# Moving key norms and norm ends from VectorE to ScalarE and GpSimd, and dealing decoding anew, in a two-layer decoder kernel

## What is computed

```python
# blocks 1 and 2: linear attention, then a selective scan gated by x
x = _layernorm(x + _L0_attn_ref(x, ...), axis=-1)
x = _layernorm(x + _L0_xattn_ref(ctx_1024, x, ...), axis=-1)   # y * silu(x)
# block 5: cross attention, 16 heads of 128
q = rmsnorm((hidden_states @ Wq).reshape(B, Sq, H, D), gq)
k = rmsnorm((encoder_hidden_states @ Wk).reshape(B, Skv, H, D), gk)
v = (encoder_hidden_states @ Wv).reshape(B, Skv, H, D)
attn = jax.nn.softmax(jnp.einsum('bqhd,bkhd->bhqk', q, k) * scale, axis=-1)
out = jnp.einsum('bhqk,bkhd->bqhd', attn, v).reshape(B, Sq, H * D) @ Wo
# block 6: feed forward whose weights are lut[idx], lut of 16 values
```

## Time and profile before

| | us |
|---|---|
| median of 3 runs | 2836.32 |
| the runs | 2829.55, 2836.32, 2836.57 |
| the profiled execution | 2836.43 |
| its span, first to last instruction | 2834.7 |
| PE busy | 2579.2 (91%) |
| DVE busy | 2044.9 (72%) |
| ACT busy | 1207.1 (43%) |
| POOL busy | 705.2 (25%) |

### The profile page before, as it was taken

The page is one execution under the profiler, slowest core; times in us unless marked ns, Lnnn a source line. Parts: engine busy times, 40 slices in busy tenths (PEclk is TensorE's granted clock), DMA queues, the critical chain, the costliest instruction groups (busy, mean ns, idle before and its releaser), DMA issues. The chain is left out here.

```text
span 2834.7 us, 29502 instructions
## 1 busy us (share of the span) xinstructions
PE 2579.2 (91%) x9938; PEld 1707.4 (60%) x9938; DVE 2044.9 (72%) x3585; ACT 1207.1 (43%) x2171; POOL 705.2 (25%) x617
## 2 busy tenths in 40 slices
PE   6998898989789789789899999999999997999997
PEld 2343433434367555566667776777777774588886
DVE  3879999899975377687868897889878895231332
ACT  3453544634433221356554555465645564021111
POOL 1445445456401156211111220111111110000000
PEclk8989999999989899899999999999999998999999
DMA  4111211112311202322323223322323215100000
GB/s 147 52 46 61 67 65 61 53 37 74 113 58 40 87 30 75 119 100 102 130 71 114 77 79 108 123 75 86 105 71 120 82 46 172 60 9 22 31 15 15
DMA packets 81568, 212.47 MB, mean 75 GB/s; under 512 B 8966, under 2 KB 17414, under 8 KB 77324
## 3 DMA queue, kind: packets, MB, share of 16 engines
q1 hardware_dynamic: 72108, 178.25, 19.0%
q0 software_dynamic: 5472, 21.01, 1.9%
q10 hardware_dynamic: 3840, 11.34, 1.1%
HBM read 164.11 MB, written 46.47 MB: 74 GB/s over the span
## 5 line engine op out<-in xcount | busy, mean ns | idle before, releaser
L2327 POOL TENSOR_TENSOR h<-du,Bb 128x1024 f32<-128x1024 f32 x128 | 312.7, 2445 | 242.6 <-DVE h L1785 240.5
L1780 DVE TENSOR_TENSOR_SCAN h<-bank,h 128x512 f32<-128x512 f32 x256 | 300.0, 1208 | 39.7 <-ACT bank L1366 32.2
L1366 ACT ACTIVATE bank<-dt,A 128x512 f32<-128x512 f32 x256 | 175.6, 690 | 317.8 <-DVE h L1780 317.1
L1554 ACT ACTIVATE p<-bank,sm,rq 128x512 f32<-128x512 f32 x256 | 199.1, 778 | 223.6 <-DVE sm L2198 223.6
L2401 POOL TENSOR_TENSOR rq<-rq,mhalf 128x4 f32<-128x4 f32 x64 | 79.4, 1241 | 819.1 <-DVE rq L2142 819.1
L694 PE MATMUL bank<-pT,v 128*128 128x512 f32 x512 | 231.2, 594 | 0.8 <-ACT pT L1257 0.8
L279 POOL TENSOR_SCALAR rstd<-mv 128x1 f32<-128x1 f32 x96 | 29.9, 312 | 788.2 <-DVE mv L273 788.2
L908 PE MATMUL bank<-h,ident 128*128 128x512 f32 x256 | 148.6, 664 | 53.9 <-DVE h L1785 53.5
L2281 DVE TENSOR_TENSOR h<-bank,sg 128x512 f32<-128x512 f32 (+1 forms) x44 | 30.4, 690 | 228.5 <-PE bank L1205 228.5
L1034 PE MATMUL bank<-x_hi,wxq_s 128*128 128x512 f32 x512 | 169.9, 414 | 23.7 <-DVE wxq_s L2154 22.0
L2194 DVE TENSOR_REDUCE sm<-bank 128x1 f32<-128x512 f32 x256 | 175.0, 684 | 7.6 <-PE bank L1034 7.4
(11 more groups left out here) (248 smaller groups left out, 6081.8 us busy)
## 6 DMA issues: line engine op xcount, KB each, us to landing
wxq_s<-wq_dram SPq DMA_DIRECT2D x48, 512.0 KB, 4.0
Bb<-bc_dram SPq DMA_DIRECT2D x32, 512.0 KB, 3.7
Cb<-bc_dram SPq DMA_DIRECT2D x32, 512.0 KB, 3.7
x_dram<-xo POOLq DMA_DIRECT2D x16, 1024.0 KB, 4.9
xc<-x_dram SPq DMA_DIRECT2D x16, 1024.0 KB, 5.3
woh<-in_Wo SPq DMA_DIRECT2D x64, 256.0 KB, 2.7
wxv_s<-wkv_dram SPq DMA_DIRECT2D x12, 1024.0 KB, 4.9
wxk_s<-wkv_dram SPq DMA_DIRECT2D x12, 1024.0 KB, 8.1
```

Of the source, the lines that this page charges most:

```text
L1366: act.activation(bank[2 + n][:, :], dt[:, c % 2, et, :], ACT.Exp, scale=A[:, et, 2 * w + n:2 * w + n + 1]).then_inc(dA_ready, 1)
L1554: act.activation(p4[:, t, :], bank[4 + t][:, :], ACT.Exp, bias=sm4[:, 4 + t:5 + t], scale=rq[:, hh % 2, 1, t:t + 1], accum_out=sm4[:, 8 + ...
L1780: dve.tensor_tensor_scan(h[:, s, n, :], bank[2 + n][:, :], h[:, s, n, :], 0.0, ALU.mult, ALU.add).then_inc(scanned, 1)
L2327: pool.tensor_tensor(h[:, G % HR, :, :], du[:, et:et + 1, :].to_broadcast([P, 2, S]), Bb[:, w % 2, :, :], ALU.mult).then_inc(dBu_ready, 1)
```

## The change

Three things are changed.

First, `key_norms` leaves DVE. ACT makes the squares with `key_squares`, one activation for each head's 128 columns of a key tile (16 for a group), each with an accumulated sum into `kss`, after all key tiles of the call are brought; a ring of six buffers takes the squares themselves. POOL adds the epsilon ahead of its power.

Second, in the heads of stage 3 the remainders of Wq, Wv and Wk in chunk 0 come ahead of the decoding, and all decoding comes behind `k_rest` and `query_mean`: masks and first pair in hh % 4 = 0; second, third, fourth pair and the next unit's masks in 1; all four pairs of the second unit in 2; none in 3. In PE's output pass `query_squares` moves from head 10 to head 11.

Third, in stage 0 `last` and `last_gated` of the chunks 0 to 2, and `last` of chunk 3, move to ACT as an Identity activation with scale and bias, at other units; POOL makes the bias by one more product (`ln_pool_shift`). The gated norm of the last chunk stays on DVE.

```diff
...
         mv = sb("mv", [P, 2, 2])
-        rstd = sb("rstd", [P, 2, 2])
+        rstd = sb("rstd", [P, 2, 4])
         mhalf = sb("mhalf", [P, 16])
...
         ln_rstd = sem("ln_rstd")
+        ln_shift = sem("ln_shift")
         ln_out = sem("ln_out")
...
+        def ln_pool_shift(pool, T, k, S):
+
+            ln_pool(pool, T, k)
+            pool.wait_ge(ln_rstd, START + T + 1)
+            hold(pool)
+            pool.tensor_scalar(rstd[:, k, 2:3], mv[:, k, 0:1], rstd[:, k, 0:1], -1.0, ALU.mult, ALU.mult).then_inc(ln_shift, 1)
+
+        def ln_last_act(act, S, k, dst):
+
+            act.wait_ge(ln_shift, START + S + 1)
+            act.activation(dst, rsum[:, k, :], ACT.Identity, scale=rstd[:, k, 0:1], bias=rstd[:, k, 2:3]).then_inc(ln_out, 1)
+
         def ln_last(dve, T, k, dst):
...
         pT = s4("pT", [P, NT, S])
-        sm4 = s4("sm4", [P, 16])
+        sm4 = s4("sm4", [P, 16]); kj = s4("kj", [P, 6, XD])
 
...
                             turn_keys(c + 1, 0)
+                        if hh == 11:
                             query_squares(c + 1, 0)
...
                 act.activation(one_e[:, :, :], one_e[:, :, :], ACT.Ln).then_inc(sp_l, 1)
+
+            def last(c, t):
+
+                act.wait_ge(stored, STORED0 + 16 * c)
+                ln_last_act(act, 8 * c + t, t % 2, x1[:, t, :])
+
+            def last_gated(c, t):
+
+                ln_last_act(act, 8 * c + 4 + t, t % 2, xo[:, t, :])
 
...
                         else:
+                            if U == 3 and c:
+                                last_gated(c - 1, 0)
+                                last_gated(c - 1, 1)
+                            if U == 5 and c:
+                                last_gated(c - 1, 2)
+                                last_gated(c - 1, 3)
+                            if U in range(28, 32):
+                                last(c, U - 28)
                             if U == 3:
...
+                        def key_squares(c, g, tiles):
+                            act.wait_ge(k_pow, START + after(c, 16, 4 * g))
+                            for t in tiles:
+                                act.wait_ge(a_done, evicted4(c, "k", g, t))
+                                for n in range(4):
+                                    m = after(c, 4 * 16, 16 * g + 4 * t + n)
+                                    act.wait_ge(k_sum, START + max(0, m - 5))
+                                    act.activation(kj[:, m % 6, :], kt4[:, t, n * XD:(n + 1) * XD], ACT.Square, scale=float(XD) ** -0.5,
+                                                   accum_out=kss[:, t, n:n + 1]).then_inc(k_sum, 1)
+
                         def values(c, g):
...
                             keys(0, 0, range(NT))
+                            key_squares(0, 0, range(NT))
                             values(0, 0)
...
                                 keys(c, hh // 4 + 1, range(NT))
+                                key_squares(c, hh // 4 + 1, range(NT))
                             if hh == 12 and c + 1 < B:
...
                                 round_out(hh)
+                                if 3 <= hh < 7:
+                                    key_squares(c + 1, 0, (hh - 3,))
                                 if hh == 10:
...
-            def last(c, t):
-                dve.wait_ge(stored, STORED0 + 16 * c)
-                ln_last(dve, after(c, 8, t), t % 2, x1[:, t, :])
-
             def gated(c):
...
                         first_gated(c - 1, 1)
-                    if U == 2 and c:
-                        last_gated(c - 1, 0)
-                        last_gated(c - 1, 1)
                     if U == 3 and c:
...
                         first_gated(c - 1, 3)
-                    if U == 4 and c:
-                        last_gated(c - 1, 2)
-                        last_gated(c - 1, 3)
                     if U == 3:
...
                         first(c, U - 26)
-                    if U in range(27, 31):
-                        last(c, U - 27)
             gated(B - 1)
...
-                        def key_norms(c, g, tiles):
-
-                            for t in tiles:
-                                n = 4 * g + t
-                                dve.wait_ge(a_done, evicted4(c, "k", g, t))
-                                dve.wait_ge(k_sum, START + after(c, 16, max(0, n - 1)))
-                                dve.wait_ge(ln_out, START + T0[3] + after(c if g else max(0, c - 1), 4, 0))
-                                dve.tensor_tensor(rsum[:, t % 2, :], kt4[:, t, :], kt4[:, t, :], ALU.mult).then_inc(k_square, 1)
-                                dve.wait_ge(k_square, START + after(c, 16, n + 1))
-                                dve.tensor_reduce(kss[:, t, :], rsum[:, t % 2, :].rearrange("p (n d) -> p n d", d=XD), AX.X, ALU.add)\
-                                    .then_inc(k_sum, 1)
-                                dve.wait_ge(k_sum, START + after(c, 16, n + 1))
-                                dve.tensor_scalar(kss[:, t, :], kss[:, t, :], 1.0 / XD, LN_EPS, ALU.mult, ALU.add).then_inc(k_mean, 1)
-
                         def key_scale(c, g):
...
                             wxq_rest(1)
-                            key_norms(0, 0, range(NT))
                             x3_rest(0, range(KD))
...
                                 q_rest(c, hh + 1)
-                            if hh % 4 == 0:
-                                masks(n)
-                            if hh % 4 == 2 and two:
-                                second_pair(n + 1)
                             if hh + 1 < XH:
...
                                 query_mean(c, hh + 1)
+                            if c == 0 and hh + 2 < XH:
+                                wxq_rest(hh + 2)
+                            if c == 0 and hh % 4 == 0 and hh // 4 + 1 < GROUPS:
+                                wxv_rest(hh // 4 + 1)
+                            if c == 0 and hh % 4 == 1 and hh // 4 + 1 < GROUPS:
+                                wxk_rest(hh // 4 + 1)
                             if hh % 4 == 0:
+                                masks(n)
                                 first_pair(n)
+                            if hh % 4 == 1:
                                 second_pair(n)
-                            if hh % 4 == 1:
                                 third_pair(n)
...
                                 masks(n + 1)
+                            if hh % 4 == 2 and two:
                                 first_pair(n + 1)
-                            if hh % 4 == 2 and two:
+                                second_pair(n + 1)
                                 third_pair(n + 1)
-                            if hh % 4 == 3 and two:
                                 fourth_pair(n + 1)
-                            if c == 0 and hh % 4 == 0 and hh // 4 + 1 < GROUPS:
-                                wxv_rest(hh // 4 + 1)
-                            if c == 0 and hh % 4 == 1 and hh // 4 + 1 < GROUPS:
-                                wxk_rest(hh // 4 + 1)
-                            if c == 0 and hh + 2 < XH:
-                                wxq_rest(hh + 2)
-                            if hh % 4 == 2 and hh // 4 < 3:
-                                key_norms(c, hh // 4 + 1, range(NT))
                             if hh == 12 and c + 1 < B:
...
                                     x3_rest(c + 1, (2, 3))
-                                if 3 <= hh < 7:
-                                    key_norms(c + 1, 0, (hh - 3,))
                                 if hh == 7:
...
                     if U in (29, 30, 31):
-                        ln_pool(pool, after(c, 8, U - 29), (U - 29) % 2)
+                        ln_pool_shift(pool, after(c, 8, U - 29), (U - 29) % 2, 8 * c + U - 29)
                     if U == 0 and c:
-                        ln_pool(pool, after(c - 1, 8, 3), 1)
+                        ln_pool_shift(pool, after(c - 1, 8, 3), 1, 8 * (c - 1) + 3)
                     if U in (4, 6) and c:
-                        ln_pool(pool, after(c - 1, 8, U), 0)
-                        ln_pool(pool, after(c - 1, 8, U + 1), 1)
+                        ln_pool_shift(pool, after(c - 1, 8, U), 0, 8 * (c - 1) + U)
+                        ln_pool_shift(pool, after(c - 1, 8, U + 1), 1, 8 * (c - 1) + U + 1)
                     if U == 8 and c:
...
                         inputs(c + 1, et)
-            for t in range(3, 8):
+            ln_pool_shift(pool, after(B - 1, 8, 3), 1, 8 * (B - 1) + 3)
+            for t in range(4, 8):
                 ln_pool(pool, after(B - 1, 8, t), t % 2)
...
                 for t in range(NT):
+                    pool.wait_ge(k_sum, START + 4 * after(c, 16, 4 * g + t + 1))
+                    hold(pool)
+                    pool.tensor_scalar(kss[:, t, :], kss[:, t, :], LN_EPS, None, ALU.add).then_inc(k_mean, 1)
                     pool.wait_ge(k_mean, START + after(c, 16, 4 * g + t + 1))
```

## The result

| | before | after |
|---|---|---|
| median of 13 runs each, us | 2832.3 | 2843.62 |
| lowest to highest | 2824.17 to 2839.29 | 2828.25 to 2849.98 |
| profiled execution's span | 2834.7 | 2845.1 |

The changed kernel takes 1.0044 of the time of the one before, 95% interval [1.0027, 1.0061]: slower by 0.44%, 11 us. The forecast was 2848.5, in a range of 2822 to 2868.

The account below looks back on a forecast made before the run. In chunks 1 to 3 PE was taken as nearly full, 59.5 of 62.8 us a group. Terms -14.6 + 2.2 - 12 + 19.8 + 17.8 - 1 = +12.2 on 2836.32 gave 2848.5 us, range 2822 to 2868.

Parts of the forecast that it names:

- key path not late: Rival, cross attention: POOL's four powers end before T+8.7, so the detour is gone; -20.6, 2816 us; chance 0.24.
- T+8.7: 8.7 us after head 7's first score (T): previous end of the fourth key_scale product, deciding whether POOL's powers come late.
- the nine groups: Groups with keys in chunks 1 to 3: later transposes and half clock cost 2.2 us each, +19.8 (+5 to +35).
- the first stage: Norm ends moved off DVE there: -14.6 us (-20 to -4).
- 1.8 a tile: POOL's addition plus power per key tile in cross attention: 1.8 us against 1.42, fourth power ending at T+9.45.
- the start of the stage: Cross stage start: 16 squares stand on ACT ahead of values and rounding of x, +2.2 us (0 to +5).
- The rival's reward: Cross attention: DVE, 6.2 us lighter, has q_lo ready when PE asks; 1.5 us a group gained, 13 in the sum.
- Part 2, tails: Last groups of chunks 1 to 3, decoding dealt anew: +7.3 in chunk 3, +5.8, +3.2, clock +1.5; +17.8 (+11 to +24).
- In heads 0 to 11 this fits: Cross attention: decoding behind k_rest fits before PE wants the next weights; heads with values or keys allow 9.6 to 9.9 us.
- Chunk 0: Its heads in cross attention: remainders ahead of decoding remove 22.0 us of PE waits; net -12 us (-20 to -4).
- the pairs' 4.8 a chunk: First stage, gated norm ends off DVE: PE starts keys 3.0 us sooner at upper clock, 4.8 a chunk, -14.4 in all.
- the boundaries: First stage chunk boundaries: one more product in ACT's chain, +1.3 us in the first, -0.25 in two, +0.8 in all.

Follow-up runs that it names:

- part 3 alone: Kernel before with only the first stage's norm ends moved to ACT and POOL; median 2817.9 us, ratio 0.9938 [0.9916, 0.9960].

## Why the prediction was right, and where it was not

**Direction and size** came out (11 us slower against 12), and of the rivals "key path not late" came nearest in its condition (its four powers did end before T+8.7), but not in its time. That the size fits is luck: the nine groups came out 10.9 below their forecast, the first stage gained 8.0 less than its forecast, the last groups cost 3.9 more than theirs, and these and smaller errors cancelled. What was right in the mechanism is the price of the new deal in the last heads.

**Part 1, the step that failed** is the term "1.8 a tile", POOL's pace. I took 1.26 to 1.42 for a power from the earlier trace rows, where four powers stood beside DVE's norms; in this head they took 1.53 once and 1.03 three times, the addition 0.22 rather than 0.33. The fourth power came at T+8.0 instead of T+9.45, below the stated T+8.7, so the +19.8 was not owed. The squares (0.33 forecast, 0.29 measured) and the start of the stage (+2.2) were right. The rival's reward, 13 us, was wrong as well: with powers at T+8.0 DVE's fourth product ends where it did, so nothing is late and nothing is gained.

**Part 2, tails**: +17.8 forecast, +21.7 measured; putting the old deal back there alone gave 22 by timing and 20.7 by the groups, chunk 0 included. The mechanism was the one named. In chunk 3 DVE's way from the end of `q_lo` to the maxima of head 15 grew by 6.4 us (5.4 to 11.8; forecast 5.4 and 1.2, 6.6), and heads 12 and 13 added 0.8 and 1.8. **Heads 0 to 11** is the second step that failed: "In heads 0 to 11 this fits". I compared decoding with PE's room in the head and left out that in heads 3, 7 and 11 four `key_scale` products stand between the maxima and the weights. The 9.9 us of head 2, 6 and 10 leave no room, the maxima come 0.9 late, and PE, which already waited 1.5 there, waits longer and drops to the lower clock. It cost +8.9 in these nine groups. This error hid the first one.

**Chunk 0**: -12 forecast, -11.3 measured, of parts that were not forecast so: -17.5 for the remainders (measured alone), +8.9 for the deal, and -2.6 without a cause shown.

**Part 3**: the pairs' 4.8 a chunk was right (4.9). The step that failed is the boundaries, "+0.8": they cost 5.7. The prediction named the longer chain on ACT but put it at 1.3 once and -0.25 twice; it was 1.9 to 2.0 each time, and ACT's wait for POOL's bias ahead of the fourth norm end (2.55 in chunk 1) was not in the sum. How much of the first stage's -14.6 was wrong stays open: by spans it is -6.6, by timing part 3 alone gives -17.5 (11 to 24) and the gated ends alone 0.70% [0.45, 0.95].

## What to carry to other kernels

Where two engines meet at a point, compute when each arrives, and price what is queued between that engine's inputs and the point: here four products between maxima and weights turned a deal that fits PE's time in the head into a late one. Work taken off an engine that is not last is worth nothing (key norms), however many microseconds it frees, and it costs where the engine that takes it over is last (ungated norm ends, 1.9 at each boundary), while the order of what is left on it was worth 39 us one way and 17 the other. Take the price of an instruction from rows where its neighbours are those that it will have.

## What the runs showed of the hardware

A DVE product of two SBUF operands that meets a POOL product lasts until 1.08 us after POOL's ends, in all 73 that took 1.30 or more in the two kernels; the others take 1.22 to 1.30.

A power of 128x4 on POOL took from 1.03 to 1.53 us in one head: 1.53 beside DVE's predicated copies and first maximum, 1.03 beside its maxima and products. In the kernel before all 56 powers of 1.24 to 1.27 lay beside decoding and all 36 of 1.42 to 1.45 beside the key norms. In the kernel with the key norms alone moved it took 1.32 where it began beside a product of DVE's. What sets this I did not find out.

The same program can pass one place at either clock level. The changed kernel and the one with the norm ends alone have the same first stage; window by window (length, busy PE, PEld, DVE, ACT, POOL, PEclk, DMA share, GB/s), the changed kernel and then the other:

```profile
180.00:190.00 10.00, 10.00 (x13) 3.21 (x12) 4.55 (x4) 3.69 (x6) 3.90 (x2) 0.57 0.00 0
```

```profile
180.00:190.00 10.00, 8.81 (x20) 3.57 (x21) 9.66 (x11) 6.66 (x9) 6.10 (x3) 1.00 0.36 106
```

At 0.57 chunk 0 of that stage took 184.6 us, at 1.00 176.9. From 169 to 190 us the granted clock was 0.59 in the changed kernel and in the one before, and 1.00 in the one with the norm ends alone; in the 6 us ahead of it PE had been busy 5.67 in all three. Units 22 to 24 of chunk 0 took 8.2 longer by it in four of the fourteen traces. The kernel before and the changed one both had it, so it is not in their difference. So a difference of some 8 us between the totals of two profiles says little by itself; the spans of groups in the cross attention, which mostly repeat to some tenths, say more.
